# Taking the three all-engine barriers out of an attention and mixture kernel

## The chip, the cores and the metric

The kernel runs on the 8 cores of one Trainium2 chip, as one program with different data on each. The metric is the device time of the slowest core in microseconds, and of several runs the median. A core has five engines with a queue of instructions each: TensorE (PE), VectorE (DVE), ScalarE (ACT), GpSimd (POOL) and SyncE (SP); the last two issue most of the transfers here. The queues run on their own and meet only at semaphores.

## The reference

For x of shape (4, 2048, 4096), with all products in the reference in 32 bits:

```python
xn = _layernorm(x, axis=-1)
# attention: q, k, v are projections of xn; 32 heads of 128, 16 key/value heads
scores = jnp.einsum('bgkqd,bkld->bgkql', q, k) * SCALE     # then the causal mask
w = jax.nn.softmax(scores, axis=-1)
s = jnp.einsum('bgkql,bkld->bgkqd', w, v)
# feed-forward: a base product plus low-rank experts, the best 2 of 8 for each row
base = jnp.einsum('bsd,od->bso', xn, base_W)
mid = jnp.einsum('bsd,edr->bser', xn, lora_A) * w_dense[..., None]
g = _silu(base + jnp.einsum('bser,erd->bsd', mid, lora_B) * SCALING)
x = x + s * g
```

## The kernel before

A pair of cores takes one batch element, each core half of its heads and output columns: 16 query heads, 8 key/value heads, 2048 columns. The program is written out by hand. `em.emit(engine, fn, waits, inc)` appends an instruction to the list of an engine (T, V, S, P, Y for PE, DVE, ScalarE, GpSimd, SyncE); the waits are put in front of it in that engine's queue, so that everything behind them in this queue waits too. Order between engines comes only from those waits and from `em.barrier`, which gives every engine a nop that increments a semaphore and then a wait for all five.

Four stages follow each other.

- Stage A (L206 to L305) loads x transposed in 32 pieces of 128 x 2048 through GpSimd's queue (L216), four in flight. ScalarE squares each piece (L222), PE sums pieces and squares against ones (L229, L235). DVE makes the rows of mean and inverse deviation (L244 to L269; the square root on ScalarE, L264), PE spreads them over the partitions (L277, L281), and DVE normalises the pieces in place, two operations each (L296, L299), each of which increments `anrm`.
- Stage B (L307 to L453) multiplies with 24 blocks of the weights of Q and K (L337): a block has 4 groups of 32 matmuls, one for each piece, its weights come through GpSimd's queue into one of two buffers (L321), ScalarE evicts each group (L346), and SyncE stores it to memory (L351). The loads of blocks 0 and 1 have no waits of their own. The router's logits (L361) and its softmax in small steps of DVE and ScalarE follow, then V in the same way (L435, L441, eviction L446, store L449).
- Stage C (L455 to L549) transposes the router's weights (L468), spreads them (L480), makes the low-rank middle (L496) and the base product with Silu (L530, L536, L542), stored to `gH` (L545) by SyncE.
- Stage D (L551 on) is the attention. DVE sets a column of ones (L560) after all stores of B and C have landed; behind it SyncE loads V (L630), K (L653) and Q (L664); PE makes scores (L694), ScalarE exponentials (L701), DVE masks (L714), PE the products with V (L596), and DVE multiplies with the gate (L742), which GpSimd adds into the output (L746).

`em.barrier` stands at L305 ("barA"), L453 ("barB") and L549 ("barC"). In the first group of stage B each matmul carries a wait of its own, for the piece that it reads:

```python
if og == 0 and ts == 0:
    wch = list(wch) + [("anrm", 2 * (ch + 1))]
```

A store or a bank is waited for by counts: `acquire("pg0")` gives the wait for the eviction of the last group that used this PSUM bank.

Of the kernel before, what the change touches and what calls it, by code (L numbers as in the profile page):

```python
# [74 lines left out]
def build_program():  # L75
# [32 lines left out]
    with ExitStack() as stack:  # L108
# [70 lines left out]
        em = Em(nc, stack)  # L179
# [7 lines left out]
        def fcnt(name):  # L187
            return ("f_" + name, em.c("f_" + name))
# [16 lines left out]
        if "A" in PHASES:  # L205
# [96 lines left out]
            if DEBUG:  # L302
                em.emit("Y", lambda E: E.dma_start(dxn[:, :], xnT[:, :]),
                        waits=[("anrm", em.c("anrm"))], inc=("dbg", 16))
            em.barrier("barA")  # L305

        if "B" in PHASES:  # L307
            def wsrc(dram, blk, width):
# [111 lines left out]
            for vog in range(4):  # L420
# [6 lines left out]
                for tc in range(16):  # L427
# [6 lines left out]
                    for ch in range(NCH):  # L434
# [15 lines left out]
                        Vs[tc * 128:(tc + 1) * 128, vog * 256:(vog + 1) * 256],  # L450
                        vstage[psl][:, :]),
                        waits=[fcnt(pname)], inc=("f_vst%d" % psl, 16))
            em.barrier("barB")  # L453

        if "C" in PHASES:  # L455
            def wsrc(dram, blk, width):
# [58 lines left out]
            for ob in range(8):  # L515
# [6 lines left out]
                for tc in range(16):  # L522
# [6 lines left out]
                    for ch in range(NCH):  # L529
# [16 lines left out]
                        gH[tc * 128:(tc + 1) * 128, ob * 256:(ob + 1) * 256],  # L546
                        gstage[psl][:, :]),
                        waits=[fcnt(pname)], inc=("f_gst%d" % psl, 16))
            em.barrier("barC")  # L549

        if "D" in PHASES:  # L551
            CBM_W = [("cbm", em.c("cbm")), ("cbu0", em.c("cbu0")),
# [288 lines left out]
```

How the kernel before makes its waits and increments, by code:

```python
    def play(self, eng, E):  # L65
        for wl, fn, il in self.ops[eng]:
            for (h, v) in wl:
                E.wait_ge(h, v)
            if fn is not None:
                ins = fn(E)
                if il is not None:
                    ins.then_inc(*il)
```

## Time and profile before

| | us |
|---|---|
| median of 2 runs | 2720.05 |
| lowest and highest of them | 2717.14, 2722.96 |
| the profiled execution | 2416.78 |
| span of its slowest core (core 6) | 2414.9 |
| spans of its eight cores | 2387.6 to 2414.9 |

The profile is that of one execution, taken on its slowest core. Its times start with the first instruction of the core. Busy time of an engine leaves out waits and the issuing of transfers. "PEclk" is the clock that TensorE was granted, as a share of 2.4 GHz. The idle time shown before an instruction carries the name of what ended it; where an instruction waited for several things that is the last of them.

### The profile page before, as it was taken

The page shows a single profiled execution, that of the slowest core. Times are in us where ns is not written, and L with a number is a line of the kernel's source. Part 1 is how long each engine was busy: PE and PEld are TensorE (multiplying, and loading weights), DVE is VectorE, ACT ScalarE, POOL GpSimd, SP SyncE. Part 2 cuts the span into 40 slices and gives each one's busy share as a digit, 9 for nine tenths or more (in the row PEclk, how much of TensorE's full clock was granted, in tenths as well). Part 3 has the DMA queues.
Part 4 walks back from the last instruction along what each step waited for, and adds up shares of the span by engine and source line. Part 5 has one row for each costly group of instructions (what it writes and reads, how often), then busy time and mean ns, then how long its engine had stood idle before and what let it go on. Part 6 is the DMA issues. An engine that isn't in the chain of part 4 may idle for free.

```text
span 2414.9 us, 33776 instructions; the slowest of 8 cores (2387.6 to 2414.9 us)
## 1 busy us (share of the span) xinstructions
PE 1826.2 (76%) x13040; PEld 1166.5 (48%) x13156; DVE 351.4 (15%) x1059; ACT 552.4 (23%) x677; POOL 93.6 (4%) x92
## 2 busy tenths in 40 slices
PE   1063209999999999947999779999998536576673
PEld 0011004444444444435888468888887224343442
DVE  0004670000000000031000100000000444334223
ACT  0063000111011101101011001111111437587783
POOL 0010000000000000000000000000000000000000
PEclk9998559999999999968999889999999569898897
DMA  9994014455444454450330153333331454535224
GB/s 159 157 169 74 0 14 54 56 59 65 55 55 55 59 67 55 64 73 14 53 53 19 21 80 71 73 73 73 71 73 42 123 120 117 120 114 106 75 75 92
DMA packets 230861, 177.97 MB, mean 74 GB/s; under 512 B 123571, under 2 KB 218932, under 8 KB 226228
## 3 DMA queue, kind: packets, MB, share of 16 engines
q0 software_dynamic: 155408, 85.53, 29.2%
q1 hardware_dynamic: 72996, 73.51, 12.1%
q10 hardware_dynamic: 2304, 16.78, 2.0%
q8 instruction: 110, 1.80, 0.3%
q14 instruction: 43, 0.35, 0.1%
HBM read 194.20 MB, written 67.11 MB: 108 GB/s over the span
## 4 chain that ended last, share of the span: by engine, by line
PE 63%; DMA 12%; DVE 9%; ACT 7%; issue 4%; another core or an unknown queue 3%; SPq 0%; DVEq 0%; POOL 0%; ACTq 0%; POOLq 0%
PE pg L337 27%; PE pg L530 19%; PE pg L435 9%; ACT arena L701 6%; DMA arena<-xT 5%; DMA out<-arena 3%; DMA arena<-Qs 2%; DVE arena L296 2%; PE pav L596 2%; DVE arena L299 2%; DVE arena L742 2%; PE pg L496 1%; DVE arena L714 1%; PE psB L694 1%
## 5 line engine op out<-in xcount | busy, mean ns | idle before, releaser
L337 PE MATMUL pg<-arena,wstr 128*128 128x512 bf16 x3010 | 661.1, 380 | 106.2 <-DMA wstr<-wqT 103.0
L337 PEld LDWEIGHTS pg<-arena,wstr 128*128 128x128 bf16 x3072 | 301.0, 98 | 467.4 <-issue 106.0
L530 PE MATMUL pg<-wstr,arena 128*128 128x256 bf16 x4096 | 463.6, 273 | 24.3 <-DMA wstr<-bwT 24.3
L530 PEld LDWEIGHTS pg<-wstr,arena 128*128 128x128 bf16 x4096 | 402.0, 98 | 72.3 <-issue 24.8
L435 PE MATMUL pg<-wstr,arena 128*128 128x256 bf16 x2048 | 238.9, 276 | 40.0 <-ACT vsb L446 40.0
L435 PEld LDWEIGHTS pg<-wstr,arena 128*128 128x128 bf16 x2048 | 197.2, 99 | 71.6 <-issue 40.1
L701 ACT ACTIVATE arena<-psA,konst 128x1024 bf16<-128x1024 f32 x160 | 178.1, 1113 | 86.5 <-PE psA L694 83.9
L701 ACT ACTIVATE arena<-psB,konst 128x1024 bf16<-128x1024 f32 x160 | 178.3, 1114 | 73.7 <-PE psB L694 64.3
L694 PE MATMUL psA<-arena 128*128 128x512 bf16 x315 | 104.7, 415 | 108.6 <-DMA arena<-Qs 75.8
L346 ACT ACTIVATE vsb<-pg,bq_sb 128x512 bf16<-128x512 f32 x64 | 44.0, 687 | 538.6 <-PE pg L337 538.6
L542 ACT ACTIVATE vsb<-pg 128x256 f32<-128x256 f32 x128 | 49.2, 384 | 407.5 <-PE pg L536 387.4
L596 PE MATMUL pav<-vsb,arena 128*128 128x129 bf16 x960 | 81.3, 235 | 70.0 <-DVE arena L714 69.7
L229 PE MATMUL psA<-arena,onec 128*1 128x512 bf16 x64 | 20.6, 406 | 146.2 <-ACT vsb L222 130.6
L596 PEld LDWEIGHTS pav<-vsb,arena 128*128 128x128 bf16 x960 | 66.2, 104 | 116.3 <-issue 107.0
L694 PE MATMUL psB<-arena 128*128 128x512 bf16 x274 | 95.7, 420 | 14.6 <-ACT arena L701 10.3
L367 DVE COPY vsb<-pav 128x8 f32<-128x8 f32 x16 | 2.7, 167 | 700.6 <-PE pav L361 700.6
L596 PEld LDWEIGHTS pg<-vsb,arena 128*128 128x128 bf16 x1216 | 84.4, 103 | 30.8 <-issue 10.4
L694 PEld LDWEIGHTS psA<-arena 128*128 128x128 bf16 x320 | 23.8, 100 | 150.6 <-issue 147.2
L596 PE MATMUL pg<-vsb,arena 128*128 128x129 bf16 x1216 | 94.3, 231 | 0.0
L222 ACT ACTIVATE vsb<-arena 128x2048 bf16<-128x2048 bf16 x32 | 61.1, 1910 | 137.9 <-DMA arena<-xT 117.0
L229 PEld LDWEIGHTS psA<-arena,onec 128*1 128x1 bf16 x64 | 3.6, 80 | 162.5 <-issue 162.5
L446 ACT ACTIVATE vsb<-pg 128x256 bf16<-128x256 f32 x64 | 24.5, 384 | 214.3 <-PE pg L441 207.0
(81 smaller groups left out, 757.8 us busy)
## 6 DMA issues: line engine op xcount, KB each, us to landing
arena<-xT POOLq DMA_DIRECT2D x32, 512.0 KB, 12.1
wstr<-wqT POOLq DMA_DIRECT2D x16, 1024.0 KB, 15.0
wstr<-bwT POOLq DMA_DIRECT2D x8, 2048.0 KB, 17.1
gH<-vsb SPq DMA_DIRECT2D x128, 128.0 KB, 1.9
arena<-gH ACTq DMA_DIRECT2D x16, 1024.0 KB, 5.6
out<-arena POOLq DMA_DIRECT2D x16, 1024.0 KB, 15.6
Qs<-vsb SPq DMA_DIRECT2D x64, 128.0 KB, 2.4
wstr<-wkT POOLq DMA_DIRECT2D x8, 1024.0 KB, 13.3
```

The source lines that it names most:

```text
L222: em.emit("S", lambda E, b=b, c=c: nc.scalar.activation(sqb[b][:, :], xnT[:, c * T:(c + 1) * T], AF.Square), waits=w, inc=("asq", 1))
L296: em.emit("V", lambda E, c=c: nc.vector.tensor_mul(xnT[:, c * T:(c + 1) * T], xnT[:, c * T:(c + 1) * T], rb_sb[:, :]), waits=w, inc=("anrm ...
L299: em.emit("V", lambda E, c=c: nc.vector.tensor_add(xnT[:, c * T:(c + 1) * T], xnT[:, c * T:(c + 1) * T], mb_sb[:, :]), waits=[("anrm", em. ...
L337: em.emit("T", lambda E, pp=pp, sl=sl, ch=ch, ts=ts: nc.tensor.matmul(pp[:, :], wbuf[sl][:, ch * 128:(ch + 1) * 128], xnT[:, ch * T + ts * ...
L346: em.emit("S", lambda E, psl=psl, pp=pp, bias=bias: nc.scalar.activation(qkstage[psl][:, :], pp[:, :], AF.Identity, bias=bias), waits=[gw, ...
L435: em.emit("T", lambda E, pp=pp, sl=sl, ch=ch, tc=tc: nc.tensor.matmul(pp[:, 0:256], xnT[:, ch * T + tc * 128: ch * T + tc * 128 + 128], vw ...
L530: em.emit("T", lambda E, pp=pp, sl=sl, ch=ch, tc=tc: nc.tensor.matmul(pp[:, 0:256], xnT[:, ch * T + tc * 128: ch * T + tc * 128 + 128], bw ...
L542: em.emit("S", lambda E, psl=psl, pp=pp: nc.scalar.activation(gstage[psl][:, :], pp[:, 0:256], AF.Silu), waits=[gw, aqs], inc=("f_" + pnam ...
L596: nc.tensor.matmul(pt[:, 0:129], wT[wsl][:, kc * 512 + qc * 128: kc * 512 + qc * 128 + 128], vslots[:, kc * 8 + i, :], start=(kc == 0), st ...
L694: nc.tensor.matmul(ps[:, uu * 512:(uu + 1) * 512], k_slot[ksl][:, kc * 128:(kc + 1) * 128], q_slot[qsl][:, :], start=True, stop=True),
L701: nc.scalar.activation(wT[wsl][:, kc0 * 512: kc0 * 512 + 1024], ps[:, 0:1024], AF.Exp, bias=konst[:, 0:1], scale=SCALE),
L742: em.emit("V", lambda E, qc=qc: nc.vector.tensor_mul(s_sb[:, qc * 2048:(qc + 1) * 2048], s_sb[:, qc * 2048:(qc + 1) * 2048], g_slot[qc][:, ...
```

## The change

The three calls of `em.barrier` behind stages A, B and C are taken out. All other instructions, their order within each queue and their waits stay as they are.

```diff
                 em.emit("Y", lambda E: E.dma_start(dxn[:, :], xnT[:, :]),
                         waits=[("anrm", em.c("anrm"))], inc=("dbg", 16))
-            em.barrier("barA")
 
         if "B" in PHASES:
...
                         vstage[psl][:, :]),
                         waits=[fcnt(pname)], inc=("f_vst%d" % psl, 16))
-            em.barrier("barB")
 
         if "C" in PHASES:
...
                         gstage[psl][:, :]),
                         waits=[fcnt(pname)], inc=("f_gst%d" % psl, 16))
-            em.barrier("barC")
```

## Rows read from the trace of the kernel before

**Rows 1.** The head of the page, and PE in 40 slices.

```profile
span 2414.9 us, 33776 instructions; the slowest of 8 cores (2387.6 to 2414.9 us)
PE 1826.2 (76%) x13040; PEld 1166.5 (48%) x13156; DVE 351.4 (15%) x1059; ACT 552.4 (23%) x677; POOL 93.6 (4%) x92
PE   1063209999999999947999779999998536576673
```

**Rows 2.** What PE waited for: us in total, times, longest us.

```profile
PE pg L337 <- DMA wstr<-wqT: 103.0, 1, 103.0
PE pg L435 <- ACT vsb L446: 40.0, 1, 40.0
```

**Rows 3.** Timeline from stage A to B: start us, us, engine, line, op [idle].

```profile
196.74 0.53 POOL L216 DMA_DIRECT2D arena<-xT  x1 [2.63 <-DMA arena<-xT]
...
209.15 1.91 ACT L222 ACTIVATE vsb<-arena 128x2048 bf16<-128x2048 bf16 x1 [0.54 <-PE psA L229]
...
213.21 1.28 DVE L244 COPY wstr<-psA 1x512 f32<-1x512 f32 x2 [211.98 <-PE pg L235]
...
264.53 1.23 DVE L296 TENSOR_TENSOR arena<-arena,vsb 128x2048 bf16<-128x2048 bf16 x1
...
348.28 1.22 DVE L299 TENSOR_TENSOR arena<-arena,vsb 128x2048 bf16<-128x2048 bf16 x1
348.89 3.38 POOL L321 DMA_DIRECT2D wstr<-wqT  x2 [151.62 <-DVEq L61]
...
366.01 24.16 PE L337 MATMUL pg<-arena,wstr 128*128 128x512 bf16 x103 [102.98 <-DMA wstr<-wqT]
```

**Rows 4.** The weight loads of L321: time from issue to landing.

```profile
DMA to landing us min/median/max: 13.0/14.9/22.4
```

**Rows 5.** Timeline at the start of stage B.

```profile
366.44 0.15 PEld L337 LDWEIGHTS pg<-arena,wstr 128*128 128x128 bf16 x1 [0.28 <-issue]
...
374.35 0.69 ACT L346 ACTIVATE vsb<-pg,bq_sb 128x512 bf16<-128x512 f32 x1 [146.72 <-PE pg L337]
...
381.26 0.69 ACT L346 ACTIVATE vsb<-pg,bq_sb 128x512 bf16<-128x512 f32 x1 [6.22 <-PE pg L337]
```

**Rows 6.** Windows: PE, PEld, DVE, ACT, POOL busy, then PEclk, DMA share, GB/s.

```profile
349.50:366.00 16.50, 0.00 (x0) 0.21 (x2) 0.00 (x1) 0.00 (x0) 2.77 (x2) 0.50 0.95 77
366.00:370.00 4.00, 3.99 (x13) 1.62 (x13) 0.00 (x0) 0.00 (x0) 0.00 (x0) 0.66 1.43 127
...
374.20:1030.00 655.80, 652.59 (x2979) 297.30 (x3039) 0.00 (x0) 65.29 (x95) 37.96 (x24) 1.00 0.48 57
1103.00:1341.00 238.00, 237.67 (x2046) 195.23 (x2045) 0.63 (x3) 23.65 (x63) 3.36 (x2) 0.99 0.21 36
1402.00:1865.00 463.00, 463.00 (x4222) 413.92 (x4220) 0.00 (x0) 50.06 (x128) 10.06 (x6) 1.00 0.35 68
```

**Rows 7.** Timeline of ScalarE at the start: pieces 0 and 1 of x.

```profile
10.82 1.28 ACT L222 ACT_TABLE_LOAD   x1 [10.82 <-DMA arena<-xT]
...
50.94 1.91 ACT L222 ACTIVATE vsb<-arena 128x2048 bf16<-128x2048 bf16 x1 [36.92 <-DMA arena<-xT]
```

**Rows 8.** Timeline of PE on core 7: the first matmul of stage B.

```profile
362.81 37.38 PE L337 MATMUL pg<-arena,wstr 128*128 128x512 bf16 x160 [101.03 <-DMA wstr<-wqT]
```

**Rows 9.** DVE's products of L742: duration ns min/median/max, first and last start.

```profile
L742 DVE TENSOR_TENSOR arena<-arena x16: 2291/2292/2294, 1953.9 to 2391.6; 128x2048 f32<-128x2048 f32 x16
```

**Rows 10.** Timeline of PE across the second barrier.

```profile
1340.39 0.28 PE L441 MATMUL pg<-bv_sb,onerb 1*128 1x256 bf16 x1
...
1342.00 1.05 PE L468 MATMUL pg<-idb,vsb 128*8 128x128 bf16 x16 [1.33 <-SPq L61]
...
1344.27 0.59 PE L480 MATMUL pav<-vsb,repl_sb 8*128 8x512 bf16 x2 [1.22 <-DVE vsb L472]
```

**Rows 11.** Timeline across the third barrier.

```profile
1868.07 0.17 DVE L560 MEMSET vsb<- 128x128 bf16 x1 [490.31 <-DMA gH<-vsb]
...
1876.90 0.63 PE L694 MATMUL psA<-arena 128*128 128x512 bf16 x1 [11.88 <-DMA arena<-Qs]
```

## The prediction, made before the changed kernel was run

> **What bounds the kernel now.** I first read the head of the page: span 2414.9 us on core 6, and TensorE (PE) busy 76% of it [rows 1]. The forty slices under it, 60 us each, show where the other 24% are. PE runs at 9 in the long middle of the projections, is mostly idle in slices 1 to 6 (stage A and its end), drops again at slices 18 and 19 and at 23 and 24, and is at 5 to 8 in stage D, where ScalarE's exponentials and DVE share the work. PE sets the pace of B and C, so whatever starts PE's dense work earlier moves the end, and whatever only lets another engine start earlier does not.
>
> Then the waits of PE between the end of stage A and the start of stage C [rows 2]. The largest is 103.0 us, put down to the weights of `wqT`; the next, 40.0 us before L435, is ScalarE working through the router's softmax and has nothing to do with a barrier. Of the barriers the trace names one at PE, 1.33 us before L468 [rows 10]. The 103.0 us needs a second look, because a wait for several semaphores is put down to the last one. The timeline of the stretch [rows 3] shows what is in it. GpSimd (POOL) issues the last piece of x at 196.74 and then stands for 151.6 us "DVEq L61", which is the wait of the first barrier. ScalarE squares the last piece at 209.15, DVE makes the row of statistics from 213.21, and the 64 normalising operations run from 264.53, one every 1.33 us, until 348.28 + 1.22 = 349.50. Only then do both weight loads start, and the first matmul of stage B starts at 366.01. Two things are therefore stacked behind the normalisation that need not be: the weight load (366.01 - 349.50 = 16.5 us) and the first group of 32 matmuls, whose eviction is at 374.35. The code already gives each of those 32 matmuls its own wait for its own piece of normalised x (L337's `anrm` wait, for the first group alone), and the barrier makes that wait idle.
>
> **The change part by part.** It takes out three barriers and adds nothing: five nops and five waits each, with every wait on data left as it was.
>
> *First barrier (barA).* POOL's next instructions are the loads of weight blocks 0 and 1, which wait for nothing. They are issued right behind the last piece of x, at about 196.74 + 0.53 = 197.3, 3.4 us for the two [rows 3]. A load of this kind lands after 13.0 to 22.4 us [rows 4], so both are there by about 197.3 + 3.4 + 22.4 = 223, which is 41 us before the first normalising operation begins. PE then works through group 0 at the pace of DVE, one matmul every 2.66 us. The last matmul waits for the operation that ends at 349.50. DVE's operations wait for each other through a semaphore and lose 1.33 - 1.23 = 0.10 us each time; for the hand-over to PE I allow 0.15 us, and a matmul in the cold clock takes 0.43 us (a weight load of 0.15 and 0.28 until the next one [rows 5]). So group 0 is done at 349.50 + 0.15 + 0.43 = 350.1. In the profile it is done when its eviction starts, 374.35 [rows 5], less a hand-over of 0.1: 374.25. That is 24.2 us earlier.
>
> Part of this has to be given back. The first matmuls of group 0 ran cold in the profile too: the granted clock is 0.50 of full (1.2 GHz) while PE idles, 0.66 over the first four microseconds and 1.00 (2.4 GHz) behind them [rows 6]. Group 0 took 374.25 - 366.01 = 8.24 us, the next one 381.26 - 374.35 = 6.91 [rows 5]; the difference, 1.3 us, is the warming-up. One matmul in 2.66 us is PE busy for 16% of the time; I take it that the clock stays low through this, so group 1 pays the same 1.3 us. **Net of barA: -24.2 + 1.3 = -22.9 us.** If the trickle of matmuls does raise the clock, it is -24.2.
>
> The cover of this saving is the early landing of the weights. If they landed late, PE would wait for them again, up to the full 16.5 us of load plus the group. What the load now runs beside is the tail of x: pieces 28 to 31 are in flight when it is issued. Both use POOL's queue. The first four pieces of x are issued together, as their code waits for nothing, and ScalarE could start on piece 0 at 10.82, with piece 1 at 50.94 [rows 7]; a queue that shared its bandwidth evenly among its loads would have landed these two close together. So the queue is served nearly in order, and the weights go behind the last piece. Lower bound 0; upper bound the longest landing of such a load, 22.4 us [rows 4], which is the second of the two. The row nearest is the pair of weight loads itself: issued together, the first let PE start 366.01 - 348.89 = 17.1 us after its issue, where the median lands in 14.9 [rows 3, 4]: some 2 us for having a neighbour, of which I take half, **+1.0 us**, on the last piece of x. DVE's row of statistics and the 64 operations then start that much later.
>
> Does PE reading x slow DVE down? The 64 operations took 1.22 to 1.23 us with PE idle [rows 3]. The trace has no such operation beside a matmul, but DVE's 128x2048 products of L742 took 2291 to 2294 ns in all 16 cases [rows 9], and at 1953.9 matmuls ran beside them. I cost it at 0, with an upper bound of one cold matmul for each piece, 32 x 0.43 = 14 us.
>
> *The Trainium skill, SBUF — State Buffer, section "SBUF: two separate sides", states that while DVE runs an operation in a 2-port mode, GpSimd cannot write the descriptors of a DMA that it issues, so the transfer appears blocked. [...] No run here shows it yet; the rival that it makes is priced below from rows.*
>
> *Second barrier (barB).* The last matmul of V starts at 1340.39; ScalarE evicts it, SP issues its store, and the eight transposes of the first half start at 1342.00, after 1.33 us of idle for SP's barrier nop [rows 10]. Their bank `pg0` was evicted one group earlier, so without the barrier they start at 1340.7 and the copy of the first half runs while the second half waits for `pg1`. I follow the chain: copy 1 from 1341.3, 0.64 us; the second half's transposes from 1341.3; copy 2 from 1341.95 to 1342.6; next matmul at 1342.9 instead of 1344.27. **-1.4 us**, between 0 and -1.5.
>
> *Third barrier (barC).* DVE's memset at 1868.07 was released by the landing of a store to `gH`, not by the barrier; the V, K and Q loads on SP's queue stand behind the memset, and PE waits for Q until 1876.90 [rows 11]. All of these waits remain in the code. **0 us**, with PE's 11.9 us wait unchanged. Bounds: 0 to -0.5.
>
> **Sum:** -22.9 + 1.0 - 1.4 + 0 = -23.3 us. The profiled execution took 2416.78 us (1.9 us lie around its span), so it would take 2393.5. The runs of the median took 2720.05, 303 us more. The sum consists of waits for DVE and DMA, which do not depend on PE's speed, and one group of matmuls, so I carry it over unchanged: 2720.05 - 23.3 = **2697 us**, -0.9%. Other cores lose a similar amount: on core 7 the first matmul stood at 362.81 [rows 8], 3.2 us before core 6's, and the end is the slowest core's.
>
> *The Trainium skill, TensorE: Matmul & The Clock Gate, section "Part 1: The HAM clock gate (the "warmup" mystery)", says that a current limiter holds a die at 13/16 of the clock once three of its cores run dense matmuls. The profile disagrees for its own execution (0.99 to 1.00 in the three long dense stretches). As an estimate by that page the three stretches, 1357 us, would take 3/13 more, 313 us, which is near the 303 us between the profiled execution and the median; and barA's group of matmuls would be worth about 1.6 us more than in my sum, 2695 us.*
>
> **The rivals.**
>
> *The weights land late anyway.* If the two loads' descriptors are not all out when DVE starts its 2048-wide operations, the load could wait until they end at 349.5, and B would start as before, at 366. For it: POOL's issue and DVE's work have never run beside each other in this stage. Against it: POOL is done issuing at 200.7 and DVE is idle until 213.21 [rows 3]. Left over is barB: 2720.05 - 1.4 + 1.0 = 2720 us. It is also the case in which the change does nothing. The skill's rule above is this rival's mechanism. 5%.
>
> *The tail of x is late.* The two weight loads share the DMA engines with pieces 28 to 31 evenly instead of going behind them. With up to 22 us of transfer between them, the statistics start 5 to 20 us later: 2702 to 2717 us. The order of landings in [rows 7] speaks against it. 7%.
>
> *Slower than before: DVE's normalisation is stretched.* Each piece's matmul reads the arena in which DVE writes. If each of 64 operations were longer by one cold matmul, 64 x 0.43 = 27.5 us, the result would be 2720.05 - 23.3 + 27.5 = 2724 us. It decides from 23.3 / 64 = 0.36 us on each operation, 1.33 to 1.70 us. The constant 2291 to 2294 ns of [rows 9] speaks against it. 3%.
>
> *The level of the runs moves.* The profiled execution lies 11% below the median, so executions of this kernel have at least two levels; if the changed kernel is timed at the lower one it is near 2393 us, or partly. Nothing in the change selects a level; against it, both timed runs agree within 0.2%. 5%.
>
> **How the numbers follow.** Forecast as worked out, gain of 15 to 30 us: 80%. The likeliest is 2697. Its own range: the unknowns are the tail of x (0 to 22, likely under 5), the clock (1.3), barB (1.4) and the spread of the timed runs (6 us). For 8 in 10 I take 2680 to 2714; the low end is a gain of 40, which allows the level of the runs to wander by half a percent, the high end a gain of 6, which takes in most of the late tail of x. About 2% is what a measurement of this kernel can tell from no change, 54 us: faster by more 4% (the level, nothing else reaches it), slower by more 1%, within it 95%.
>
> **What would show each step.** In the profile after: POOL's two L321 loads at about 197 instead of 348.9; the first L337 matmul at about 267, then one every 2.66 us; the eviction of group 0 at about 351 instead of 374.35; L296 and L299 still at 1.23 us; PE's 103.0 us wait for `wqT` gone, with waits for DVE in its place; the last L222 within 1 or 2 us of 209.15; transposes of L468 at once behind L441; the wait for Q before L694 still 11.9 us. The prediction is wrong if the last L222 slips by more than 5 us, if the first dense group starts after 355, or if a stage behind it grows by what the first one gains.

## The result: 0.9% faster, and the profile after

| | before | after |
|---|---|---|
| median of all runs | 2431.33 us (14 runs) | 2405.99 us (15 runs) |
| lowest and highest | 2412.71, 2722.96 us | 2395.16, 2549.28 us |
| the profiled execution | 2416.78 us | 2406.12 us |
| spans of the eight cores | 2387.6 to 2414.9 us | 2383.5 to 2404.2 us |

The ratio of after to before is 0.9914, with a 95% interval of 0.9886 to 0.9942. Of 2431 us that is 21 us less (14 to 28). It is a small gain, well inside 2%, and the measurement can just tell it from none.

In some executions of either kernel the cores of one die are granted a lower TensorE clock and take up to 13% longer (in one of the kernel before, core 4 took 2721 us at a mean clock of 0.769 and core 1 2408 us at 0.891); the two runs of 2717 and 2723 us shown ahead of the prediction were as long as that, and all ratios here are worked out without such executions.

The head of the page of the changed kernel, core 1:

```profile
span 2404.2 us, 33862 instructions; the slowest of 8 cores (2383.5 to 2404.2 us)
PE 1849.5 (77%) x13156; PEld 1167.6 (49%) x13156; DVE 351.0 (15%) x1059; ACT 552.5 (23%) x677; POOL 93.6 (4%) x92
...
PE   1063339999999999929999599999997546576773
```

Against [rows 1], which is of core 6, slice 5 went from 2 to 3 and slice 6, in which PE was idle, from 0 to 3. That is group 0, run in single matmuls, and the dense work that now starts before 360 us. From here on core 6 is shown, the one that the rows of before are from; it went from 2414.9 to 2392.4 us. Its timeline from stage A to B (L320, L336 and L345 are L321, L337 and L346 of before):

```profile
197.86 3.39 POOL L320 DMA_DIRECT2D wstr<-wqT  x2
...
208.75 1.91 ACT L222 ACTIVATE vsb<-arena 128x2048 bf16<-128x2048 bf16 x1 [0.61 <-PE psA L229]
...
264.12 1.23 DVE L296 TENSOR_TENSOR arena<-arena,vsb 128x2048 bf16<-128x2048 bf16 x1
...
266.79 0.10 PEld L336 LDWEIGHTS pg<-arena,wstr 128*128 128x128 bf16 x1 [5.75 <-issue]
...
269.48 0.59 PE L336 MATMUL pg<-arena,wstr 128*128 128x512 bf16 x1 [6.86 <-DVE arena L299]
...
347.87 1.23 DVE L299 TENSOR_TENSOR arena<-arena,vsb 128x2048 bf16<-128x2048 bf16 x1
...
349.24 36.11 PE L336 MATMUL pg<-arena,wstr 128*128 128x512 bf16 x154 [2.07 <-DVE arena L299]
...
349.97 0.69 ACT L345 ACTIVATE vsb<-pg,bq_sb 128x512 bf16<-128x512 f32 x1 [122.75 <-PE pg L336]
...
358.74 0.69 ACT L345 ACTIVATE vsb<-pg,bq_sb 128x512 bf16<-128x512 f32 x1 [8.08 <-PE pg L336]
...
365.64 0.69 ACT L345 ACTIVATE vsb<-pg,bq_sb 128x512 bf16<-128x512 f32 x1 [6.22 <-PE pg L336]
```

GpSimd issues the two weight loads directly behind the last piece of x, at 197.86, where it stood at 348.89 in [rows 3]. The first operation of the normalisation starts at 264.12, and from 266.8 on there is a single matmul every 2.66 us. (The trace holds no record of the first matmul; its weight load stands at 266.79.) The last one starts at 349.24, 0.14 us after DVE's last operation ends (347.87 + 1.23). Group 0 is evicted at 349.97 instead of 374.35 [rows 5], group 1 at 358.74 instead of 381.26. Group 1 took 8.8 us from one eviction to the next, group 2 6.9: the warming-up is now in group 1. PE's waits (us in total, times, longest):

```profile
PE pg L336 <- DVE arena L299: 69.1, 31, 6.9
...
PE pg L434 <- ACT vsb L445: 41.1, 1, 41.1
...
PE pg L528 <- DMA wstr<-bwT: 25.8, 1, 25.8
```

The 103.0 us for `wqT` of [rows 2] have become 31 short waits for DVE. The 40 us wait behind the router is as it was, and so is one for the first weights of the base product (`bwT`), 25.8 us here and 24.3 before. The windows of the same stretch, with the columns of [rows 6]:

```profile
264.50:349.50 85.00, 17.79 (x31) 3.39 (x33) 78.02 (x64) 0.00 (x0) 0.00 (x0) 0.50 0.00 0
349.50:355.00 5.50, 5.50 (x18) 2.08 (x18) 0.00 (x0) 0.69 (x1) 0.00 (x0) 0.64 0.07 24
355.00:1005.00 650.00, 646.79 (x2952) 294.68 (x3012) 0.00 (x0) 64.61 (x94) 37.97 (x24) 1.00 0.49 58
```

The granted clock stayed at 0.50 during the single matmuls (17.8 us busy of 85) and rose within the next 5.5 us.

PE across the place of the second barrier, and the timeline across that of the third:

```profile
1317.68 0.28 PE L440 MATMUL pg<-bv_sb,onerb 1*128 1x256 bf16 x1
1317.89 1.36 PE L466 MATMUL pg<-idb,vsb 128*8 128x128 bf16 x16
1320.28 0.59 PE L478 MATMUL pav<-vsb,repl_sb 8*128 8x512 bf16 x2 [1.04 <-DVE vsb L470]
```

```profile
1840.75 0.27 PE L534 MATMUL pg<-vsb 128*128 128x256 bf16 x1
...
1844.07 0.17 DVE L557 MEMSET vsb<- 128x128 bf16 x1 [491.29 <-DMA gH<-vsb]
...
1853.48 0.63 PE L691 MATMUL psA<-arena 128*128 128x512 bf16 x1 [12.46 <-DMA arena<-Qs]
```

From the last matmul of V to the spreading of the router's weights it is 1320.28 - 1317.68 = 2.60 us, against 3.88 in [rows 10]. The wait for Q of [rows 11] is still there, 12.46 us for 11.88.

So the gain of core 6 can be followed along its span. It is 24.4 us at the end of group 0, 22.5 at the end of group 1, 22.7 at the last matmul of V, 24.0 behind the second barrier's place, 23.4 at the first scores, and 22.5 at the end.

Core 6 is one of the cores on which it can be followed to the end; not all are like it. Group 0's eviction is 23.4 to 27.7 us earlier on every core, but from the first scores to the end the eight cores took 524 to 541 us in the profiled execution before and 536 to 549 us in the one after. So the end moves by anything from 24.5 us earlier (core 7) to 13.8 us later (core 0). No run here shows what lengthens the attention in one execution and not in another. The 0.9% rests on the ratio of all those runs, and not on this pair of profiles.

### The profile page after: what moved, and what is told of

Read it like the earlier page. It is cut to its first block, busy times and chain, and to the rows that moved or that the text cites. A ratio compares the mean times of both kernels' runs of the same rounds, so it can differ in the third digit from the quotient of the medians.

```text
span 2404.2 us, 33862 instructions; the slowest of 8 cores (2383.5 to 2404.2 us)
## 1 busy us (share of the span) xinstructions
PE 1849.5 (77%) x13156; PEld 1167.6 (49%) x13156; DVE 351.0 (15%) x1059; ACT 552.5 (23%) x677; POOL 93.6 (4%) x92
## 4 chain that ended last, share of the span: by engine, by line
PE 64%; DMA 12%; DVE 9%; ACT 7%; issue 4%; another core or an unknown queue 3%; SPq 0%; DVEq 0%; POOL 0%; ACTq 0%; POOLq 0%
PE pg L336 27%; PE pg L528 18%; PE pg L434 9%; ACT arena L698 6%; DMA arena<-xT 5%; DMA out<-arena 3%; DMA arena<-Qs 2%; PE pav L593 2%; DVE arena L296 2%; DVE arena L299 2%; DVE arena L739 2%; PE psB L691 1%; DVE arena L711 1%; PE pg L494 1%
## 5 line engine op out<-in xcount | busy, mean ns | idle before, releaser
L336 PE MATMUL pg<-arena,wstr 128*128 128x512 bf16 x3072 | 676.7, 382 | 68.5 <-DVE arena L299 68.5
L336 PEld LDWEIGHTS pg<-arena,wstr 128*128 128x128 bf16 x3072 | 301.2, 98 | 445.0 <-issue 87.5
L434 PEld LDWEIGHTS pg<-wstr,arena 128*128 128x128 bf16 x2048 | 197.3, 99 | 72.0 <-issue 40.4
L345 ACT ACTIVATE vsb<-pg,bq_sb 128x512 bf16<-128x512 f32 x64 | 44.0, 687 | 516.5 <-PE pg L336 516.5
L691 PE MATMUL psB<-arena 128*128 128x512 bf16 x320 | 106.6, 418 | 10.5 <-ACT arena L698 8.9
L445 ACT ACTIVATE vsb<-pg 128x256 bf16<-128x256 f32 x64 | 24.5, 384 | 215.0 <-PE pg L440 201.4
## 6 DMA issues: line engine op xcount, KB each, us to landing
wstr<-bwT POOLq DMA_DIRECT2D x8, 2048.0 KB, 22.7
```

What stands on the lines that cost most here:

```text
L336: em.emit("T", lambda E, pp=pp, sl=sl, ch=ch, ts=ts: nc.tensor.matmul(pp[:, :], wbuf[sl][:, ch * 128:(ch + 1) * 128], xnT[:, ch * T + ts * ...
L345: em.emit("S", lambda E, psl=psl, pp=pp, bias=bias: nc.scalar.activation(qkstage[psl][:, :], pp[:, :], AF.Identity, bias=bias), waits=[gw, ...
L434: em.emit("T", lambda E, pp=pp, sl=sl, ch=ch, tc=tc: nc.tensor.matmul(pp[:, 0:256], xnT[:, ch * T + tc * 128: ch * T + tc * 128 + 128], vw ...
L691: nc.tensor.matmul(ps[:, uu * 512:(uu + 1) * 512], k_slot[ksl][:, kc * 128:(kc + 1) * 128], q_slot[qsl][:, :], start=True, stop=True),
```

## Experiments

Times are the ratio to the kernel before, measured beside it on one chip for each group: e1, e2, e3 and e5 together, e4, e6, e7 and e8 together, e9 alone. The changed kernel was in none of these groups: where a run is compared with it in time, its ratio of 0.9914 from the result is used.

### The first barrier alone

```diff
-            em.barrier("barA")
```

> The kernel before without its first barrier only. Theory (two terms of the first barrier carry the gain: the weight load brought forward and group 0 run during the normalisation): -22 us against before, ratio 0.991, the second barrier's wait of 1.3 us before the transposes still there. Rival (each barrier costs about the same, a third of the measured 21 us): -7 us, ratio 0.997.

Measured: 0.9928 (0.9904 to 0.9953), 17 us less. Core 6, the first operation of the normalisation, group 0's eviction, and PE at the second barrier:

```profile
266.00 1.23 DVE L296 TENSOR_TENSOR arena<-arena,vsb 128x2048 bf16<-128x2048 bf16 x1
...
351.85 0.69 ACT L345 ACTIVATE vsb<-pg,bq_sb 128x512 bf16<-128x512 f32 x1 [122.75 <-PE pg L336]
...
1321.97 0.28 PE L440 MATMUL pg<-bv_sb,onerb 1*128 1x256 bf16 x1
1323.57 1.05 PE L467 MATMUL pg<-idb,vsb 128*8 128x128 bf16 x16 [1.33 <-SPq L61]
```

The distance that matters is from the first normalising operation to the eviction of group 0: 351.85 - 266.00 = 85.85 us here, 349.97 - 264.12 = 85.85 in the changed kernel, and 374.35 - 264.53 = 109.8 before. The first barrier alone therefore gives all of the 24.0 us of the changed kernel at this point. The second barrier's 1.33 us of idle is where [rows 10] had it. The rival, each barrier a third, is out: its ratio of 0.997 lies outside the interval.

### The second and third barrier alone

```diff
-            em.barrier("barB")
...
-            em.barrier("barC")
```

> The kernel before without its second and third barrier, the first one kept. Theory: -1.4 us, ratio 0.999 to 1.000; the chain of the transposes 1.4 us shorter, the wait for Q at the start of stage D unchanged at 12 us. Rival (each barrier costs about the same): -14 us, ratio 0.994.

Measured: 1.0010 (0.9983 to 1.0036). The rival's 0.994 is out; a gain of 1.4 us can't be told from none in the time. PE on core 6:

```profile
349.15 3.38 POOL L321 DMA_DIRECT2D wstr<-wqT  x2 [150.72 <-DVEq L61]
...
369.14 11.04 PE L337 MATMUL pg<-arena,wstr 128*128 128x512 bf16 x43 [105.83 <-DMA wstr<-wqT]
...
1343.99 0.28 PE L441 MATMUL pg<-bv_sb,onerb 1*128 1x256 bf16 x1
...
1346.59 0.59 PE L479 MATMUL pav<-vsb,repl_sb 8*128 8x512 bf16 x2 [1.04 <-DVE vsb L471]
...
1874.60 1.01 PE L692 MATMUL psA<-arena 128*128 128x512 bf16 x2 [12.12 <-DMA arena<-Qs]
```

The chain from V's last matmul to the spreading is 1346.59 - 1343.99 = 2.60 us, the same 2.60 as in the changed kernel and 1.28 less than before. The wait for Q is still 12.12 us. What can cover the 1.3 us in the measured time is in the first two rows: in this execution the weights came 369.14 - 349.15 = 20.0 us after their issue, and in that of [rows 3] 17.1 (over the eight cores 15.1 to 21.3 and 15.2 to 19.0). The load that the first barrier puts on the path varies by more than the second barrier costs.

### The loads ahead of the first barrier, all barriers kept

```diff
+            for og in range(2):
+                r = wqT.rearrange("(c p) n -> p c n", p=128)
+                em.emit("P", lambda E, og=og, r=r: E.dma_start(
+                    wbuf[og].rearrange("p (c n) -> p c n", n=128),
+                    r[:, :, og * 128:(og + 1) * 128]), inc=("bw%d" % og, 16))
             em.barrier("barA")
...
+                if og >= 2:
                     em.emit("P", lambda E, d=dram, ogl=ogl, sl=sl: E.dma_start(
```

> The kernel before with all three barriers, but the loads of weight blocks 0 and 1 issued ahead of the first one. This takes the load out of the path and leaves group 0 behind the normalisation. Theory: the first matmul of stage B follows the barrier at once, about 350 us instead of 366, so -16.5 us, ratio 0.993; group 0's eviction near 358. Rival (the overlap of group 0 with the normalisation is what counts, the load would be hidden by itself or is delayed by DVE): -7 us or less, ratio 0.997.

Measured: 0.9948 (0.9919 to 0.9978), 13 us less. The interval holds both expectations, so the time does not decide; the trace of core 6 does:

```profile
200.18 3.40 POOL L307 DMA_DIRECT2D wstr<-wqT  x2
...
266.52 1.23 DVE L296 TENSOR_TENSOR arena<-arena,vsb 128x2048 bf16<-128x2048 bf16 x1
...
350.76 11.41 PE L343 MATMUL pg<-arena,wstr 128*128 128x512 bf16 x45 [85.74 <-DVEq L61]
...
359.52 0.69 ACT L352 ACTIVATE vsb<-pg,bq_sb 128x512 bf16<-128x512 f32 x1 [129.89 <-PE pg L343]
```

Group 0 starts at 350.76, released by the barrier, and no longer by the weights. From the first normalising operation to the eviction it is 359.52 - 266.52 = 93.0 us, 16.8 less than before (expected 16.5). The changed kernel's 85.85 is 7.15 less again. These are the two terms of the first barrier: 16.8 for the load, 7.2 for group 0 behind the normalisation, of which group 1 pays back 1.9 in the low clock.

### The loads issued while DVE normalises

```diff
-                w = [] if og < 2 else [("bwu%d" % sl, og // 2)]
+                w = [("anrm", 1)] if og < 2 else [("bwu%d" % sl, og // 2)]
```

(on the changed kernel)

> The changed kernel, but the loads of weight blocks 0 and 1 wait for the first normalising operation, so that GpSimd issues them while DVE works through its 64 operations. Theory (the load is not hindered by DVE): they land 15 to 23 us after their issue, the first matmul is near 285 us, PE catches up with DVE, and group 0 ends where it does in the changed kernel: ratio to before 0.991. Rival (the Trainium skill, SBUF - State Buffer: GpSimd cannot write descriptors while DVE holds the shared port): the landing takes many times as long, up to the end of the normalisation at 349.5; then group 0 starts only there or later, and the time is near that of before, ratio 0.999.

Measured: 0.9932 (0.9909 to 0.9955), as the theory had it; the rival's 0.999 is outside. Core 6:

```profile
265.97 1.23 DVE L296 TENSOR_TENSOR arena<-arena,vsb 128x2048 bf16<-128x2048 bf16 x1
...
267.76 3.39 POOL L320 DMA_DIRECT2D wstr<-wqT  x2 [68.12 <-DVE arena L296]
...
285.61 3.57 PE L336 MATMUL pg<-arena,wstr 128*128 128x512 bf16 x8 [21.15 <-DMA wstr<-wqT]
289.93 0.38 PE L336 MATMUL pg<-arena,wstr 128*128 128x512 bf16 x1 [0.75 <-DVE arena L299]
...
351.81 0.69 ACT L345 ACTIVATE vsb<-pg,bq_sb 128x512 bf16<-128x512 f32 x1 [122.75 <-PE pg L336]
```

The loads are issued at 267.76 with 62 of DVE's 64 operations still to come, and PE starts at 285.61, 17.85 us later. Over the eight cores it is 14.4 to 20.7 us; without DVE beside them the same loads took 15.2 to 19.0 us before and 15.1 to 21.3 us in e2. Then PE works off the eight pieces that are ready in 3.6 us and goes on at DVE's pace. Group 0's eviction stands 85.84 us behind the first operation, the same as in the changed kernel. And DVE's operations (duration in ns, min/median/max):

```profile
L299 DVE TENSOR_TENSOR arena<-arena,vsb x32: 1224/1225/1225, 267.3 to 349.7; 128x2048 bf16<-128x2048 bf16 x32
```

The Trainium skill, SBUF — State Buffer, section "SBUF: two separate sides", has DVE lock out GpSimd's descriptor writing while it runs an operation in a 2-port mode, and this run's rival took the normalisation for such work. The same page, in its section "Who interferes with whom", gives `tensor_tensor` no 2-port mode, and the rows call these operations TENSOR_TENSOR. So the rule was never about them, and the trace agrees: the loads were no slower beside them. What it would do to operations in a 2-port mode no run here shows. The early place of the loads behind the last piece of x is not needed; an issue at 267.76 served as well.

### Weights of the base product early

```diff
-                w = list(MGT) if ob < 2 else [("cbu%d" % sl, ob // 2)]
+                w = [("bvu%d" % sl, 2)] if ob < 2 else [("cbu%d" % sl, ob // 2)]
```

(on the changed kernel)

> The changed kernel, with the loads of the first two base-weight blocks of stage C waiting for their buffers only (the last V groups that read them), not for the low-rank middle. Theory (the place of the second barrier was cheap because this wait on data behind it holds the loads back anyway): the 24 us wait of PE for these weights goes, ratio to before 0.991 - 0.010 = 0.981. Rival (the transfer collides with the stores of V, or PE waits for something else there): under half of it, ratio 0.987 or more.

Measured: 0.9827 (0.9771 to 0.9883). PE's waits on core 4:

```profile
PE pg L434 <- ACT vsb L445: 41.1, 1, 41.1
...
PE pg L528 <- DVE vsb L503: 0.9, 1, 0.9
```

The 25 us for `bwT` are down to 0.9 for DVE. The measured point is 21 us below the changed kernel's, near the theory's 0.981, but the interval reaches the rival's 0.987 too; it is the trace that says that the wait is gone. In the changed kernel, without any barrier, GpSimd issued these loads at 1353.59 us on this core, behind a wait for DVE's low-rank middle (`MGT`); here they go out at 1256.70 and 1317.77. So a wait on data behind the second barrier held the same loads back by itself, and that is why taking out the barrier alone did not bring them forward.

### More groups during the normalisation

The changed kernel with block 0's four groups piece by piece, one bank each (`pg0`, `pg1`, `pav0`, `pav1`); `NOG` is 1 here and 2 in the next run:

```diff
+            for ch in range(NCH):
+                for g in range(4 * NOG):
+                    og, ts = g // 4, g % 4
...
+                    if g == 0:
+                        w = w + [("anrm", 2 * (ch + 1))]
+                    gws[g] = mm_w(og, ts, ch, banks8[g][0], w)
```

> The changed kernel, with all four groups of weight block 0 run piece by piece during the normalisation, in four banks of PSUM. Four cold matmuls of 0.43 us for each piece are 1.7 us of DVE's 2.66. Theory: three more groups of 6.9 us are hidden: -20 us against the changed kernel, ratio to before 0.983. Rival (DVE slows down once PE reads x most of the time): the normalisation takes longer than 85 us and the gain is under 10 us, ratio 0.987 or more.

Measured: 0.9813 (0.9765 to 0.9861), near the expected 0.983; the rival's 0.987 is just outside. The window of the normalisation on core 5:

```profile
264.50:349.50 85.00, 58.16 (x125) 13.65 (x126) 77.97 (x64) 0.00 (x0) 0.00 (x0) 0.50 0.00 0
```

PE was busy 58.2 us of 85 and was granted 0.50 all the same. DVE's 64 operations took 77.97 us, as beside single matmuls (78.02). With eight groups, the halves of psA and psB as further banks, and four weight buffers:

> The changed kernel, with all eight groups of weight blocks 0 and 1 run piece by piece during the normalisation, in all eight banks of PSUM, and four weight buffers. Eight matmuls for each piece are 3.4 us at the low clock and 1.7 us at the high one, against 2.66 us of DVE. Theory: PE is busy enough for the high clock, seven more groups are hidden: -47 us against the changed kernel, ratio to before 0.972. Rival (the clock stays at its low level): PE needs 32 x 3.4 = 109 us from 267, ends at 376 instead of 350 and gains 48 - 26 = 22 us, ratio 0.982.

Measured: 0.9804 (0.9754 to 0.9855). The two windows of the normalisation on core 5, and DVE's operations:

```profile
264.50:300.00 35.50, 26.03 (x104) 9.71 (x104) 32.69 (x28) 0.00 (x0) 2.13 (x2) 0.93 0.72 60
300.00:349.50 49.50, 35.02 (x149) 13.30 (x150) 44.55 (x37) 0.53 (x1) 0.00 (x0) 1.00 0.00 0
```

```profile
L299 DVE TENSOR_TENSOR arena<-arena,vsb x32: 1224/1225/1226, 264.7 to 347.1; 128x2048 bf16<-128x2048 bf16 x32
```

The clock did rise, to 0.93 and 1.00, and DVE was not slowed, so the theory's mechanism held, and the rival's low clock is out. Still the gain over the changed kernel was 27 us of the expected 47, and the ratio is that of four groups: the four further groups, hidden as they are, brought nothing that the times show. ScalarE's evictions behind the normalisation, and PE's next start:

```profile
348.97 1.26 ACT L350 ACTIVATE vsb<-pg,bq_sb 128x512 bf16<-128x512 f32 x2 [122.55 <-PE pg L337]
353.83 1.26 ACT L350 ACTIVATE vsb<-pav,bq_sb 128x512 bf16<-128x512 f32 x2 [3.60 <-DMA Qs<-vsb]
369.00 1.31 ACT L350 ACTIVATE vsb<-psA,bq_sb 128x512 bf16<-128x512 f32 x2 [13.90 <-DMA Qs<-vsb]
380.89 1.26 ACT L350 ACTIVATE vsb<-psB,bq_sb 128x512 bf16<-128x512 f32 x2 [10.59 <-DMA Qs<-vsb]
...
386.01 54.23 PE L337 MATMUL pg<-arena,wstr 128*128 128x512 bf16 x244 [21.86 <-ACT vsb L350]
```

The eight groups end together. ScalarE has two staging slots, and its evictions from 353.83 on wait for stores of Q to land; these took up to 14.4 us from issue to landing, with weight loads under way beside them, where the median is 2.2. Single stores took nearly as long in the kernel before (up to 13.2), but there PE never had to wait for an eviction of these groups. PE waited 21.9 us for the eviction at 385.18. The missing 20 us of the gain became a new wait.

### All of it, and the new wait taken away

e8 has the eight groups, the early base weights, and the router's softmax for each block of 128 rows behind that block's first V eviction instead of ahead of all of them:

```diff
-            for tc in range(16):
+            def route(tc):
                 sl8 = lgn[:, tc * 8:(tc + 1) * 8]
...
                         waits=[fcnt(pname)], inc=("f_vst%d" % psl, 16))
+                    if vog == 0:
+                        route(tc)
```

> The eight groups, the early base weights, and the router's softmax interleaved with the evictions of the first 16 V groups on ScalarE, instead of ahead of them. Theory (the three waits are independent): 47 + 24 + 38 us less than the changed kernel, ratio to before 0.946. Rival (V's groups now wait for ScalarE behind the softmax of each row block, 2.5 us against a group of 3.8, or a later stage takes the gain back): 0.955 or more.

Measured: 0.9511 (0.9453 to 0.9569), 2303.64 us median. The interval holds both the expected 0.946 and the rival's 0.955, so the time does not decide between them. In the trace of core 7 PE's 40 us wait behind the router and the 25 us for `bwT` are gone, and a wait of 16.7 us for the evictions remains (13.9 to 19.6 over the cores). The router's edit was not run alone, so what it is worth by itself is not shown.

e9 gives the first eight groups staging slots of their own:

```diff
+                if slot is not None:
+                    st = vsb[:, 512 * slot:512 * slot + 512]
...
+                        Qs[og, :, ts * 512:(ts + 1) * 512], st),
+                        waits=[fcnt(pname)], inc=("st8", 16))
...
-            em.emit("P", lambda E: E.dma_start(lA_sb[:, :], lAi[:, :]), inc=("cld", 16))
+            em.emit("P", lambda E: E.dma_start(lA_sb[:, :], lAi[:, :]), waits=[("st8", 128)], inc=("cld", 16))
```

> The version with all three edits, plus eight staging slots of their own for the first eight groups, so that ScalarE can evict them one behind the other without waiting for a store to land. In the version with eight groups PE waited 21.9 us once, and with all three edits 16.7 us, for evictions that themselves waited for stores of Q to land while two weight loads were under way. Theory: this wait goes, -15 us against the version with all three edits, ratio to before 0.945. Rival (the stores are held up by the loads anyway and PE waits a few groups later for the same queue): no change, ratio 0.951.

Measured: 0.9479 (0.9442 to 0.9517), 2292.01 us median. The evictions on core 3:

```profile
349.17 1.27 ACT L348 ACTIVATE vsb<-pg,bq_sb 128x512 bf16<-128x512 f32 x2 [122.48 <-PE pg L337]
350.33 1.27 ACT L348 ACTIVATE vsb<-pav,bq_sb 128x512 bf16<-128x512 f32 x2
351.47 1.29 ACT L348 ACTIVATE vsb<-psA,bq_sb 128x512 bf16<-128x512 f32 x2
352.61 1.31 ACT L348 ACTIVATE vsb<-psB,bq_sb 128x512 bf16<-128x512 f32 x2
357.65 0.69 ACT L359 ACTIVATE vsb<-pg,bq_sb 128x512 bf16<-128x512 f32 x1 [3.73 <-PE pg L337]
```

They now follow each other without a wait, and PE goes on without one, so the rival's wait "a few groups later" did not appear at PE. The point is 8 us below e8's, half of what was expected, and the intervals of the two overlap; that the wait is gone is shown, what it was worth is not. e9 is 5.2% faster than the kernel before, six times the 0.9% that taking out the barriers gave.

## Why the prediction was right and where it was wrong

The predicted time, 2697 us, was wrong: the changed kernel's median is 2406, far below the range of 2680 to 2714. The change itself was forecast well: 2697 / 2720.05 is 0.9915, measured 0.9914 (0.9886 to 0.9942). That the fourth digit agrees is luck: the same 23.3 us set against the 2431 us that the kernel before really takes would be 0.9904, which the interval holds as well.

**The step that failed is the last line of the sum**, "I carry it over unchanged: 2720.05 - 23.3". The term that was mis-sized is the 2720.05 us that stood for the kernel before: over 14 runs its median is 2431.33, and 11 of the 14 were below 2460. I had a profiled execution of 2416.78 us and two runs of 2720, and took the two for the rule and the one for the exception, since they were called the median. The rival "the level of the runs moves" had the right arithmetic, "near 2393 us", and got 5%, with "both timed runs agree within 0.2%" against it. That two runs agree says little about how often their time occurs. The profiled execution was as good a witness as either of them. With the three as equals, a third of the chance belonged near 2393, and the range had to say so.

What gave those two runs their 303 us more stays open. The prediction's estimate for it, 313 us, was by the current limiter of the Trainium skill, TensorE: Matmul & The Clock Gate (section "Part 1: The HAM clock gate (the "warmup" mystery)"). The page's condition, three cores of a die in dense matmuls, also held in the profiled execution before, and there all eight cores were granted 0.98 to 1.00 in the three dense stretches. So the condition alone does not decide it.

**The first barrier: right.** Loads at 197.86 (forecast 197.3), group 0 done by 349.97 (350.1), the gain 24.4 us (24.2). Group 1 gave back 8.77 - 6.91 = 1.9 us, forecast 1.3. Net 22.5 against 22.9. (Group 1 gave back 2.7 us in e1 and 1.6 in e5, so this term varies by a microsecond.) e3 splits it as the steps did, 16.8 (forecast 16.5) and the rest.

**The tail of x: mis-sized, a little.** I charged +1.0 us. The first normalising operation starts at 263.8 us on average over the eight cores of the changed kernel and at 263.7 before. In the runs measured together it is 265.5 in e1 and 266.1 in e3, which have the loads early, and 265.3 in e2 and 265.6 in e5, which have them late. So it is between nothing and 0.7 us, less than the 1.6 us by which two executions with late loads differ (263.7 and 265.3), and the rival with 5 to 20 us is out.

The reading of [rows 7] left something out. Piece 1 came 40 us after piece 0 while four copies of `xsel` to `out` were under way on SP's queue (L199, 16.8 MB together). They were issued by 6.9 us and the last took 115.1 us to land. ScalarE squared pieces 1, 2 and 3 at 50.94, 98.25 and 121.31 us, and from then on one piece every 3 us. That four loads issued together came one behind the other still speaks for the order that the prediction took. But in these first 121 us PE is busy for 10.7 and the DMA engines for 97%: that is more time than all three barriers held, and no run here moved the copies. As an estimate from these rows, four pieces at 3 us each would take 12 of the 121 us. What of that could be had is not shown.

**DVE beside PE: right at 0.** The operations stayed at 1.23 us with one matmul beside each pair, and with eight (1224 to 1226 ns in e7).

**The starved loads: out**, and for a stronger reason than the one given. I argued that DVE is idle while the loads are issued. e5 shows that it would not have mattered: I had applied a rule for 2-port modes to operations that the same page gives none.

**The second barrier: right**, 1.28 us of 1.4 in the chain, in the changed kernel, and in e2 with the first barrier kept. It can't be seen in the time.

**The third barrier: right at 0.** The wait for Q stayed; it is 12.46 for 11.88 us on core 6, which took back 0.6 us. It is 12.12 in e2 and 11.86 in e1, so it varies by that much from one execution to the next.

Two readings of [rows 1] were off without bearing on the sum: PE is at 6 in slice 3, so it is not idle through slices 1 to 6, and in stage D it falls to 3 twice.

## What to carry to other kernels

A barrier costs what stands behind it and could have been elsewhere: look in each queue at the first instruction behind it and ask what that one waits for by itself. Here one of three barriers held a load and a group of matmuls that were free to go, 24 us; the other two stood in front of waits on data that ended as late or nearly so (1.3 us and 0). The larger waits were ordinary ones with no barrier in sight: a load that waits for more than its buffer, evictions queued behind another engine's chain.

When single executions of one kernel differ by 11%, as the profiled one and the two timed runs did here, forecast the ratio, and give each of the times seen a chance of its own.

## What the hardware showed that was not expected

- With bursts of four matmuls every 2.66 us (e6) PE was busy 58.2 us of 85, and the granted clock stayed at 0.50 (1.2 GHz). With bursts of eight (e7) PE was granted 0.93 over the first 35.5 us and 1.00 (2.4 GHz) behind them. PE waited as long for DVE between two bursts in both, 0.79 and 0.77 us. The eight groups of e7 took 61 us of busy time in this stretch, the four of e6 58 us, so twice the matmuls cost PE 3 us more.
- GpSimd's loads went at their usual pace beside DVE's bf16 `tensor_tensor` operations of 128x2048: 14.4 to 20.7 us from issue to first use over the eight cores, against 15.1 to 21.3 without them.
- A store of 128 KB through SP's queue has a median of 2.2 us to landing in e7 and 2.4 before, and single ones took up to 14.4 and 13.2 us. The long ones of e7 stood beside weight loads of 1 MB each; that these are the cause is not shown.
